# Returned ranks through PSUM, longer DMA runs, row requests four slots ahead, and SP two experts ahead in an attention and mixture-of-experts kernel

## The chip, the cores and the metric

The kernel runs on one core of a Trainium2 chip. The metric is the device time of one execution in microseconds (us); lower is better. Before the change three runs gave 371.84, 372.33 and 375.02, median 372.33 us.

## What is computed

`x` is [4, 256, 256], 1024 tokens of 256 values in all. The reference does two residual steps:

```python
x = x + xattn(layernorm(x), ctx)     # both operands rounded to fp8 by blocks of 128, then multiplied
x = x + moe(layernorm(x))            # 64 experts of width 176, top 8 for each token, and a shared expert of width 352
```

In `moe` a router scores 64 experts, keeps four of eight groups and then the eight best experts of a token. Each expert computes `silu(x Wg) * (x Wu)` and multiplies it by `Wd`; the eight results of a token are weighted and added, and the shared expert is added too.

## The kernel before, in words

The work has three parts, written as one program for each engine (SP, POOL, ACT, DVE, PE) with semaphores between them.

*Front.* Attention, layer norm, router, shared expert. The kernel then sorts tokens by expert. A token's eight experts in ascending order are its *ranks* 0 to 7. POOL scatters the token rows (256 values and 64 weights) into the DRAM buffer `xs`, rank by rank, with eight indirect DMAs a rank (line 477); after each rank it counts `ranks_in` up (line 469).

*Slot loop* (lines 591, 917, 1110). A *slot* is up to 128 rows of one expert; with these inputs there are 84 slots, in 21 groups of four (*quads*). In the iteration of slot j:

- ACT copies the transposed intermediate (594) and the high half of the rows (286), waits for SP to announce the gate/up weights (602), computes silu of slot j+1 (604), copies the high half of the weights of slot j+3 (304), and asks for the rows of slot j+AHEAD (`load_rows`, 556), if enough ranks are stored; AHEAD is 5. In the first iteration of a quad it stores the y of the quad before to `ys` (588).
- PE turns the rows of slot j+2 (1089), turns the intermediate of slot j (1120), does gate and up of slot j+1 (1095, six products) and down of slot j (1134).
- DVE makes the low halves (314, 308), multiplies silu by up (321) and scales y (930).
- SP goes by experts, in rings of four places (360 to 407). It waits until a place is free, loads the gate/up weights of the expert after, announces the gate/up weights that it loaded before, loads the down weights and announces the earlier ones. For each it reads an expert's number and a slot number into registers (361, 364).

*Tail.* POOL gathers the results of each rank back from `ys` with eight indirect DMAs (493), as soon as the last quad that holds the rank is stored, in the order of ranks. DVE adds ranks 0 to 6 to `fin`, each as one operation over 2048 columns (939), and the last rank in four quarters (944); SP stores each quarter to the output (411).

Results lie in `ys` by slot and row: `yidx` (886) holds for each token and rank its row there.

Of the kernel before, what the change touches and what calls it, by code (L numbers as in the profile page):

```python
# [5 lines left out]
def xattn_moe_kernel(  # L6
# [22 lines left out]
    I = w_down.shape[1]  # L29
# [24 lines left out]
    AHEAD = 5  # L54
    COLS = R * (QUADS + 1) + AHEAD
    ROWS = T * TOPK
    QROWS = R * P
    FILLS = QUADS * R // C
# [4 lines left out]
    with ctx:  # L63
# [93 lines left out]
        yos8 = sb("yos8", [P, C, 8])  # L157
        sidx = sb("sidx", [P, C, 8], i32)
        yidx = sb("yidx", [P, C, 8], i32)
        slot_ge = sb("slot_ge", [E, COLS])  # L160
        used_ge = sb("used_ge", [E, E + 1])
# [7 lines left out]
        used_tab = sb("used_tab", [1, E + 1], i32)  # L169
        first_tab = sb("first_tab", [1, E + 1], i32)  # L170
# [63 lines left out]
        top_ok, top_ps, max_ok, max_ps, ranks_ok = (sem(n) for n in ("top_ok", "top_ps", "max_ok", "max_ps", "ranks_ok"))  # L234
        y_sum, done = sem("y_sum"), sem("done")
# [28 lines left out]
        def load_down(eng, e, r):  # L264
            eng.dma_start(d_ring[:, r, :, :], w_down[bass.ds(e, 1), :, :].rearrange("a (s p) h -> p (a s) h", p=I0)).then_inc(d_in[r], 16)
# [5 lines left out]
        SLOT_ROWS = [(0, COLS), (COLS, COLS), (2 * COLS, E + 1), (2 * COLS + E + 1, E + 1)]  # L271
        assert 2 * COLS + 2 * (E + 1) <= 512
# [67 lines left out]
        def _(sp):  # L340
# [19 lines left out]
            def used_expert(n):  # L360
                return sp.value_load(used_tab[0:1, bass.ds(n, 1)], min_val=0, max_val=E - 1)  # L361

            def first_slot(n):
                return sp.value_load(first_tab[0:1, bass.ds(n, 1)], min_val=1, max_val=MAX_SLOTS)  # L364
# [5 lines left out]
            experts = [used_expert(r) for r in range(3)]  # L370
            for r in range(3):
                load_gu(sp, experts[r], r)
            announce(gu_in, 0, 1, gu_there)
            experts.append(used_expert(3))
            load_down(sp, experts[0], 0)
            announce(gu_in, 1, 1, gu_there)
            load_gu(sp, experts[3], 3)
            load_down(sp, experts[1], 1)
            announce(gu_in, 2, 1, gu_there)
            announce(d_in, 0, 1, down_there)  # L380
            load_down(sp, experts[2], 2)
            announce(gu_in, 3, 1, gu_there)
            announce(d_in, 1, 1, down_there)
            load_down(sp, experts[3], 3)
            announce(d_in, 2, 1, down_there)

            e, first = used_expert(R), first_slot(1)
            rings = sp.value_load(sizes[0:1, 1:2], min_val=0, max_val=E // R - 1)
            quads = quads_of(sp)
            sp.wait_ge(glo_ok, first)  # L390
            load_gu(sp, e, 0)
            with sp.Fori(0, E // R - 1) as i:
                with sp.If(i < rings):
                    e, first = used_expert(i * R + R), first_slot(i * R + 1)
                    for r in range(R):


                        e_next, first_next = used_expert(i * R + (R + r + 1)), first_slot(i * R + (r + 2))
                        sp.wait_ge(glo_ok, first_next)
                        load_gu(sp, e_next, (r + 1) % R)  # L400
                        announce(gu_in, r, i + 2, gu_there)
                        sp.wait_ge(out_ps, first)
                        load_down(sp, e, r)
                        announce(d_in, (r - 1) % R, i + (1 if r == 0 else 2), down_there)
                        e, first = e_next, first_next
            announce(gu_in, 0, rings + 2, gu_there)
# [92 lines left out]
        def _(act):  # L499
# [115 lines left out]
            store_quad(quads, bass.ds((quads + 1) % 2, 1))  # L615
# [570 lines left out]
```

## Time and profile before

| what | before |
|---|---|
| median of 3 runs | 372.33 us |
| the profiled execution | 372.08 us |
| its span, first to last instruction | 370.1 us |
| PE busy | 267.1 us (72%) |
| DVE busy | 267.0 us (72%) |
| ACT busy | 168.5 us (46%) |
| POOL busy | 165.6 us (45%) |
| slot loop, first to last y (line 930) | 113.2 to 334.4 us |
| DMA, mean over the span | 233 GB/s |

Times in the rows below are counted from the span's start. In a timeline a row has start, duration, engine, line, operation, tiles, how many were merged, and in brackets the engine's idle time before it and what ended it. An engine's name with q is its sequencer: it issues DMAs and loads registers while the engine computes. "issue" is waiting for nothing that the profile shows.

### The profile page before, as it was taken

What the parts mean: (1) busy time and instruction counts of PE and PEld (TensorE: products, weight loads), DVE (VectorE), ACT (ScalarE), POOL (GpSimd) and SP (SyncE); (2) the same over time, 40 slices, a digit from 0 to 9 for tenths busy, and PEclk for the clock granted to TensorE, in tenths of its full rate; (3) what the DMA queues carried; (4) which work ended last, traced back from release to release, by engine and by line L of the source; (5) the groups of instructions that cost most, each with busy time, mean ns of one, the idle gap of its engine ahead of it and who ended that gap; (6) DMA issues with size and microseconds to landing.
All of it is one profiled execution on the core that took longest, in us unless ns stands there. A gap on an engine that the chain in (4) does not pass through costs nothing.

```text
span 370.1 us, 7966 instructions
## 1 busy us (share of the span) xinstructions
PE 267.1 (72%) x1431; PEld 217.3 (59%) x1432; DVE 267.0 (72%) x640; ACT 168.5 (46%) x407; POOL 165.6 (45%) x164
## 2 busy tenths in 40 slices
PE   0101479979959499999999996898999989990000
PEld 0001165444748388888888885687888878880000
DVE  4799779996436268888887885565788887888832
ACT  1071542310126156667766764455676666660000
POOL 5015410427777778770000000445302773788882
PEclk9999999998979889999999999798999999997555
DMA  7999960004967479799757796898948899774134
GB/s 236 409 425 428 425 265 3 0 0 141 339 236 252 159 257 333 252 299 283 228 177 245 213 273 192 263 280 257 298 128 269 265 309 294 217 224 136 57 118 137
DMA packets 49241, 86.23 MB, mean 233 GB/s; under 512 B 5676, under 2 KB 38220, under 8 KB 47180
## 3 DMA queue, kind: packets, MB, share of 16 engines
q1 hardware_dynamic: 18652, 41.10, 32.0%
q10 hardware_dynamic: 24432, 26.12, 22.3%
q0 software_dynamic: 6144, 18.88, 15.3%
q14 instruction: 10, 0.08, 0.1%
q8 instruction: 3, 0.05, 0.1%
HBM read 46.07 MB, written 40.01 MB: 233 GB/s over the span
## 4 chain that ended last, share of the span: by engine, by line
PE 35%; DMA 13%; issue 12%; POOL 11%; DVE 10%; SPq 4%; POOLq 1%; ACT 1%; ACTq 1%; DVEq 1%
PE bank L1095 14%; PE bank L1134 13%; POOL xs L477 7%; PE bank L1120 4%; PE bank L1089 3%; DMA d_ring<-w_down 3%; DMA rows<-xs 3%; DMA early_c<-w_gu 3%; POOL xw L493 2%; POOL s_int L493 2%; SPq L361 1%; DMA xs<-xw,sidx 1%; SPq L364 1%; DVE gtop L778 1%; DMA ys<-y 1%
## 5 line engine op out<-in xcount | busy, mean ns | idle before, releaser
L1134 PE MATMUL bank<-d_ring,early_c 88*128 x336 | 93.8, 404 | 6.4 <-ACT early_c L594 5.3
L308 DVE TENSOR_TENSOR gu_lo<-early_c,gu_hi 128x704 fp32r<-128x704 f32 x87 | 76.9, 884 | 1.0 <-ACT gu_hi L304 0.6
L477 POOL DMA_INDIRECT xs<-xw,sidx x64 | 66.1, 1033 | 24.1 <-issue 23.2
L493 POOL DMA_INDIRECT early<-ys,yidx x24 | 26.2, 1094 | 102.4 <-DMA ys<-y 96.0
L1134 PEld LDWEIGHTS bank<-d_ring,early_c 88*128 88x128 f32 x336 | 60.5, 198 | 19.0 <-issue 12.6
L304 ACT ACTIVATE gu_hi<-early_c 128x704 fp32r x87 | 68.0, 782 | 5.9 <-issue 5.8
L930 DVE TENSOR_SCALAR y<-bank,rows 128x256 f32<-128x256 f32 x84 | 40.6, 483 | 34.2 <-PE bank L1134 32.7
L1095 PE MATMUL bank<-gu_hi,r_hi 128*128 128x352 f32 x170 | 63.8, 375 | 0.7 <-DVE r_lo L314 0.7
L1095 PE MATMUL bank<-gu_hi,r_lo 128*128 128x352 f32 x170 | 56.2, 331 | 0.0
L1095 PE MATMUL bank<-gu_lo,r_hi 128*128 128x352 f32 x170 | 56.1, 330 | 0.0
L594 ACT ACTIVATE early_c<-bank 88x256 f32<-88x256 f32 x84 | 31.9, 380 | 49.9 <-PE bank L1120 34.0
L604 ACT ACTIVATE early_t<-bank 128x176 f32<-128x176 f32 x84 | 26.6, 317 | 39.2 <-PE bank L1095 26.6
L314 DVE TENSOR_TENSOR r_lo<-bank,r_hi 128x256 fp32r<-128x256 f32 x86 | 36.0, 419 | 10.6 <-ACT r_hi L286 9.5
L321 DVE TENSOR_TENSOR early_t<-early_t,bank 128x176 f32<-128x176 f32 x85 | 28.5, 336 | 19.4 <-ACT early_t L604 15.2
L1089 PE MATMUL bank<-ident,rows 128*128 128x128 f32 x172 | 34.4, 282 | 6.3 <-DMA rows<-xs 5.8
L1120 PE MATMUL bank<-ident,early_t 128*88 128x128 f32 x168 | 33.8, 284 | 6.7 <-DVE early_t L321 6.4
L1089 PEld LDWEIGHTS bank<-ident,rows 128*128 128x128 f32 x172 | 24.4, 147 | 17.9 <-DMA rows<-xs 6.5
L286 ACT ACTIVATE r_hi<-bank 128x256 fp32r<-128x256 f32 x86 | 32.0, 372 | 4.4 <-PE bank L1089 4.4
L1095 PEld LDWEIGHTS bank<-gu_hi,r_hi 128*128 128x128 f32 x170 | 33.3, 196 | 1.1 <-issue 0.9
L1095 PEld LDWEIGHTS bank<-gu_lo,r_hi 128*128 128x128 f32 x170 | 33.5, 197 | 0.0
L1095 PEld LDWEIGHTS bank<-gu_hi,r_lo 128*128 128x128 f32 x170 | 33.0, 194 | 0.0
L1004 PE MATMUL bank<-xfT,sgu_sb 128*128 128x512 f32 (+1 forms) x48 | 24.9, 673 | 0.5 <-ACT scores L547 0.5
(199 smaller groups left out, 291.3 us busy)
## 6 DMA issues: line engine op xcount, KB each, us to landing
ys<-late SPq DMA_DIRECT2D x16, 1024.0 KB, 23.4
rows<-xs ACTq DMA_DIRECT2D x89, 160.0 KB, 3.3
early_c<-w_gu SPq DMA_DIRECT2D x37, 352.0 KB, 3.9
ys<-y ACTq DMA_DIRECT2D x22, 512.0 KB, 4.2
d_ring<-w_down SPq DMA_DIRECT2D x36, 176.0 KB
xc<-x SPq DMA_DIRECT2D x2, 512.0 KB, 4.0
xc<-ctx_kn SPq DMA_DIRECT2D x1, 1024.0 KB, 9.3
xs<-xw,sidx POOLq DMA_INDIRECT x64
```

What stands on the lines that cost most here:

```text
L286: act.activation(r_hi[:, b, :, :], XT[b][:, 0:H].rearrange("p (k t) -> p k t", k=KB), ACT.Copy).then_inc(rhi_ok, 1)
L304: act.activation(gu_hi[:, b:b + 1, :], gu_ring[:, bass.ds(nth % R, 1), :], ACT.Copy).then_inc(ghi_ok, 1)
L308: v.tensor_tensor(gu_lo[:, b:b + 1, :], gu_ring[:, bass.ds(nth % R, 1), :], gu_hi[:, b:b + 1, :].bitcast(fp32), ALU.subtract).then_inc(glo ...
L314: v.tensor_tensor(r_lo[:, b, :, :], XT[b][:, 0:H].rearrange("p (k t) -> p k t", k=KB), r_hi[:, b, :, :].bitcast(fp32), ALU.subtract).then_ ...
L477: pool.indirect_dma_start(out=xs, out_offset=bass.IndirectOffsetOnAxis(ap=sidx[:, c, at:at + 1], axis=0), in_=xw[:, c, :], in_offset=None, ...
L493: pool.indirect_dma_start(out=back[k][:, c, :], out_offset=None, in_=ys, in_offset=bass.IndirectOffsetOnAxis(ap=yidx[:, c, at:at + 1], axi ...
L594: act.activation(iT[:, r % 2, :, :], IT[r % 2][0:I0, 0:2 * P].rearrange("p (s t) -> p s t", s=2), ACT.Copy).then_inc(iT_ok, 1)
L930: v.tensor_scalar(y[:, odd, r, :], OB[r % 2][:, 0:H], rows[:, place, bass.ds(expert + H, 1)], None, ALU.mult).then_inc(y_ok, 1)
L1089: ins = pe.transpose(XT[b][:, k * P:(k + 1) * P], rows[:, r, k * P:(k + 1) * P], ident[:, :])
L1095: ins = pe.matmul(GB[b][:, 0:GU], r[:, b, k, :], gu[:, b, k * GU:(k + 1) * GU], start=(s == 0), stop=(s == len(parts) - 1))
L1120: ins = pe.transpose(IT[b][0:I0, s * P:(s + 1) * P], inter[:, b, s * I0:(s + 1) * I0], ident[:, :])
L1134: ins = pe.matmul(OB[b][:, 0:H], iT[:, b, s, :], d_ring[:, place, s, :], start=(s == 0), stop=(s == 1))
```

## The change

1. DRAM layouts. `w_down` is stored so that a partition reads one run of 512 values in place of two of 256. In `ys` a quad's rows lie partition by partition, so that a partition writes one run of four rows. The row of a token in `ys` then needs its slot and its quad, which `home_rows` computes on DVE just before the loop; the single operation of line 886 goes.
2. AHEAD is 4, and the request for rows stands before the copy of the weights' high half.
3. SP loads the gate/up weights of the expert after next (LEAD is 2), and reads the numbers of a ring of four with three loads of several registers. A table `gu_first_tab` is made for it on DVE.
4. The sum of the returned ranks: PE adds ranks 0 and 1 into four PSUM banks by a product with the identity; ACT copies ranks 2 to 6, in quarters, into four other banks; DVE adds the quarters from the banks to `fin`; the last rank is added from SBUF by quarters as before.

```diff
-    AHEAD = 5
+    AHEAD = 4
...
-            eng.dma_start(d_ring[:, r, :, :], w_down[bass.ds(e, 1), :, :].rearrange("a (s p) h -> p (a s) h", p=I0)).then_inc(d_in[r], 16)
+            eng.dma_start(d_ring[:, r, :, :], w_down[bass.ds(e, 1), :, :].rearrange("a p (s h) -> p (a s) h", s=2)).then_inc(d_in[r], 16)
...
+            for n in range(LEAD):
+                sp.wait_ge(glo_ok, after_slot(gu_firsts[n]))
+                load_gu(sp, number(sp, used[n]), n)
+            announce(gu_in, 0, 2, gu_there)
             with sp.Fori(0, E // R - 1) as i:
                 with sp.If(i < rings):
-                    e, first = used_expert(i * R + R), first_slot(i * R + 1)
+                    sp.load(used, used_tab[0:1, bass.ds(i * R + R, R + LEAD)])
+                    sp.load(firsts, first_tab[0:1, bass.ds(i * R + 1, R)])
+                    sp.load(gu_firsts, gu_first_tab[0:1, bass.ds(i * R + 1, R + LEAD)])
                     for r in range(R):
-                        e_next, first_next = used_expert(i * R + (R + r + 1)), first_slot(i * R + (r + 2))
-                        sp.wait_ge(glo_ok, first_next)
-                        load_gu(sp, e_next, (r + 1) % R)
-                        announce(gu_in, r, i + 2, gu_there)
-                        sp.wait_ge(out_ps, first)
-                        load_down(sp, e, r)
+                        sp.wait_ge(glo_ok, after_slot(gu_firsts[r + LEAD]))
+                        load_gu(sp, number(sp, used[r + LEAD]), (r + LEAD) % R)
+                        announce(gu_in, (r + 1) % R, i + (3 if r == R - 1 else 2), gu_there)
+                        sp.wait_ge(out_ps, after_slot(firsts[r]))
+                        load_down(sp, number(sp, used[r]), r)
                         announce(d_in, (r - 1) % R, i + (1 if r == 0 else 2), down_there)
...
-                act.dma_start(ys[bass.ds(quad * QROWS, QROWS), :].rearrange("(r p) h -> p r h", p=P),
+                act.dma_start(ys[bass.ds(quad * QROWS, QROWS), :].rearrange("(p r) h -> p r h", r=R),
...
+                    load_rows(starts[odd][r], waiteds[odd][r], (odd * R + r + AHEAD) % RING)
                     weights_high(act, nth, (r + 1) % 2)
-                    load_rows(starts[odd][r], waiteds[odd][r], (odd * R + r + AHEAD) % RING)
...
+            for k in range(PE_RANKS, TOPK - 1):
+                act.wait_ge(back_in[k], C * 16)
+                for q in range(LAST):
+                    if k > PE_RANKS:
+                        act.wait_ge(plane_sum, (k - PE_RANKS - 1) * LAST + q + 1)
+                    act.activation(bank[LAST + q][:, :].rearrange("p (c h) -> p c h", c=CL), back[k][:, q * CL:(q + 1) * CL, :],
+                                   ACT.Copy).then_inc(plane_ps, 1)
...
-            v.tensor_scalar(yidx[:, :, :], yos8[:, :, :], QROWS - 1.0, None, ALU.add).then_inc(home_ok, 1)
...
+            def home_rows():
+
+                whole(y_slot, yos8, P, -1)
+                whole(y_quad, y_slot, R, 0)
+                step(v.tensor_scalar(yos8[:, :, :], yos8[:, :, :], float(R), QROWS - float(R), ALU.mult, ALU.add))
+                step(v.tensor_scalar(y_quad[:, :, :], y_quad[:, :, :], float(QROWS - R), None, ALU.mult))
...
-            for k in range(TOPK - 1):
-                v.wait_ge(back_in[k], C * 16)
-                step(v.tensor_tensor(fin[:, :, :], fin[:, :, :], back[k], ALU.add))
-                settle()
...
+            for k in range(PE_RANKS, TOPK - 1):
+                for q in range(LAST):
+                    v.wait_ge(plane_ps, (k - PE_RANKS) * LAST + q + 1)
+                    if k > PE_RANKS:
+                        v.wait_ge(plane_sum, (k - PE_RANKS - 1) * LAST + q + 1)
+                    add_half(q, turned(LAST + q)).then_inc(plane_sum, 1)
+            for q in range(LAST):
+                v.wait_ge(low_ranks_ps, q + 1)
+                v.wait_ge(plane_sum, (TOPK - 2 - PE_RANKS) * LAST + q + 1)
+                step(add_half(q, turned(q)))
...
+            for k in range(PE_RANKS):
+                pe.wait_ge(back_in[k], C * 16)
+            for q in range(LAST):
+                for k in range(PE_RANKS):
+                    ins = pe.matmul(bank[q][:, :], ident[:, :], back[k][:, q * CL:(q + 1) * CL, :].rearrange("p c h -> p (c h)"),
+                                    start=(k == 0), stop=(k == PE_RANKS - 1))
+                ins.then_inc(low_ranks_ps, 1)
```

`whole` is two operations that round to a whole number by adding and subtracting a large constant; `home_rows` ends in two more operations that put `yidx` together.

## Rows read from the trace of the kernel before

**Rows 1.** Page, the chain that ended last, shares of the span by engine

```profile
PE 35%; DMA 13%; issue 12%; POOL 11%; DVE 10%; SPq 4%; POOLq 1%; ACT 1%; ACTq 1%; DVEq 1%
```

**Rows 2.** Timeline, one undisturbed iteration: start us, us, engine, line, op, tiles, count

```profile
328.71 0.38 PE L1089 MATMUL bank<-ident,rows 128*128 128x128 f32 x2
...
330.37 0.32 ACT L604 ACTIVATE early_t<-bank 128x176 f32<-128x176 f32 x1 [0.37 <-PE bank L1095]
...
330.88 0.34 ACTq L556 DMA_DIRECT2D rows<-xs  x1
...
330.99 0.38 PE L1089 MATMUL bank<-ident,rows 128*128 128x128 f32 x2
```

**Rows 3.** Lines 930 and 1089 in three stretches: count, ns min/median/max, first and last start

```profile
L930 DVE TENSOR_SCALAR y<-bank,rows x11: 482/483/484, 310.2 to 333.9; 128x256 f32<-128x256 f32 x11
...
L1089 PE MATMUL bank<-ident,rows x134: 270/274/421, 133.3 to 305.1; 128*128 128x128 f32 x134
...
L1089 PE MATMUL bank<-ident,rows x156: 270/274/421, 133.3 to 331.1; 128*128 128x128 f32 x156
```

**Rows 4.** DMA issues from 265 to 330 (last number: us to landing); line 556, 140 to 330

```profile
rows<-xs ACTq DMA_DIRECT2D x27, 160.0 KB, 3.3
...
DMA to landing us min/median/max: 2.1/3.7/6.1
```

**Rows 5.** Waits from 204 to 262: who waited for whom, us, times, longest

```profile
ACT early_t L604 <- SPq L368: 11.9, 7, 2.9
```

**Rows 6.** SP's and ACT's register loads (lines 361, 364, 300); line 262, 204 to 260

```profile
L361 SPq TENSOR_LOAD <-used_tab x45: 264/437/1782, 87.6 to 305.6; - x45
...
L364 SPq TENSOR_LOAD <-first_tab x41: 262/270/1342, 102.9 to 306.4; - x41
...
L300 ACTq TENSOR_LOAD <-quad_tab x69: 307/314/911, 94.3 to 331.8; - x69
...
DMA to landing us min/median/max: 3.6/4.3/6.1
```

**Rows 7.** Timeline at slot 8 and at slot 74

```profile
126.08 0.34 ACTq L556 DMA_DIRECT2D rows<-xs  x1
...
126.66 0.38 ACT L594 ACTIVATE early_c<-bank 88x256 f32<-88x256 f32 x1 [6.10 <-POOLq L469]
...
133.34 0.38 PE L1089 MATMUL bank<-ident,rows 128*128 128x128 f32 x2
...
304.94 0.44 PE L1089 MATMUL bank<-ident,rows 128*128 128x128 f32 x2 [1.09 <-DMA rows<-xs]
```

**Rows 8.** Timeline of the tail; line 493, the gathers into s_int

```profile
312.50 1.01 POOL L493 DMA_INDIRECT xc<-ys,yidx  x1 [5.45 <-DMA ys<-y]
...
333.91 0.48 DVE L930 TENSOR_SCALAR y<-bank,rows 128x256 f32<-128x256 f32 x1 [0.57 <-PE bank L1134]
...
335.88 0.42 ACTq L588 DMA_DIRECT2D ys<-y  x1
...
336.23 6.94 DVE L939 TENSOR_TENSOR x<-x,early 128x2048 f32<-128x2048 f32 x3 [1.04 <-issue]
336.40 3.02 POOL L493 DMA_INDIRECT s_int<-ys,yidx  x1 [0.30 <-issue]
...
365.93 0.69 DVE L944 TENSOR_TENSOR x<-x,xw 128x512 f32<-128x512 f32 x1 [2.15 <-DMA xw<-ys,yidx]
...
L493 POOL DMA_INDIRECT s_int<-ys,yidx x8: 1007/2018/3015, 335.1 to 351.3; - x8
```

**Rows 9.** Groups by line: count, busy us, mean ns of one, idle before

```profile
L1004 PE MATMUL bank<-xfT,sgu_sb 128*128 128x512 f32 (+1 forms) x48 | 24.9, 673 | 0.5 <-ACT scores L547 0.5
...
L830 DVE TENSOR_TENSOR pos<-bank,offset 128x512 f32<-128x512 f32 x1 | 0.7, 690 | 0.0
...
L542 ACT ACTIVATE xfT<-bank 128x512 f32<-128x512 f32 x4 | 2.3, 596 | 5.5 <-PE bank L979 5.5
...
L886 DVE TENSOR_SCALAR yidx<-yos 128x64 int32<-128x64 f32 x1 | 0.3, 317 | 0.1
```

More of the change, by code:

```diff
@@ L28, in xattn_moe_kernel @@
     E = gate_kn.shape[1]
-    I = w_down.shape[1]
+    I = 2 * w_down.shape[1]
     GU = 2 * I
@@ L358, in _, with after_slot @@
             sp.wait_ge(regs_ok, 1)
[L360 to L364, printed above, removed]
+            LEAD = 2
+            used = [sp.alloc_register(f"sp_used{n}") for n in range(R + LEAD)]
+            firsts = four_registers(sp, "sp_first")
+            gu_firsts = [sp.alloc_register(f"sp_gu_first{n}") for n in range(R + LEAD)]
+            quad_used = four_registers(sp, "sp_quad_used")
+            def after_slot(register):
+                return sp.snap(register, min_val=0, max_val=2 * P - 1) & (2 * P - 1)
             def announce(loaded, place, loads, there):
@@ L368, in announce @@
                 sp.sem_inc(there, 1)
-            experts = [used_expert(r) for r in range(3)]
+            sp.load(quad_used, used_tab[0:1, 0:R])
             for r in range(3):
-                load_gu(sp, experts[r], r)
+                load_gu(sp, number(sp, quad_used[r]), r)
+            load_down(sp, number(sp, quad_used[0]), 0)
             announce(gu_in, 0, 1, gu_there)
-            experts.append(used_expert(3))
-            load_down(sp, experts[0], 0)
+            load_gu(sp, number(sp, quad_used[3]), 3)
@@ L404, in _ @@
                         announce(d_in, (r - 1) % R, i + (1 if r == 0 else 2), down_there)
-                        e, first = e_next, first_next
-            announce(gu_in, 0, rings + 2, gu_there)
+            announce(gu_in, 1, rings + 2, gu_there)
             announce(d_in, R - 1, rings + 1, down_there)
@@ L847, in _ @@
             step(v.tensor_copy(cum_col[:, :], bank[1][0:E, CUM:CUM + 2]))
+            step(v.tensor_copy(slots[:, :], bank[1][0:1, TOTAL:TOTAL + 1]))
             step(v.tensor_scalar(quads_f[:, 0:1], bank[1][0:1, TOTAL:TOTAL + 1], 1.0 / R, (R - 1.0) / R - 0.375, ALU.mult, ALU.add))
@@ L908, in _ @@
                     weights_low(v, number(v, first_nths[f]), f, f + 1)
+            home_rows()
             quads = quads_of(v)
@@ L936, in _, with add_half, turned @@
             v.wait_ge(sh_fin, C)
-            for k in range(TOPK - 1):
-                v.wait_ge(back_in[k], C * 16)
-                step(v.tensor_tensor(fin[:, :, :], fin[:, :, :], back[k], ALU.add))
-                settle()
-            for a in range(LAST):
-                cs = slice(a * CL, (a + 1) * CL)
-                v.wait_ge(final_in[a], CL * 16)
-                v.tensor_tensor(fin[:, cs, :], fin[:, cs, :], back[TOPK - 1][:, cs, :], ALU.add).then_inc(y_sum, 1)
+            sums = [0]
+            def add_half(q, what):
+                ins = v.tensor_tensor(fin[:, q * CL:(q + 1) * CL, :], fin[:, q * CL:(q + 1) * CL, :], what, ALU.add)
+                sums[0] += 1
+                return ins
+            def turned(q):
+                return bank[q][:, :].rearrange("p (c h) -> p c h", c=CL)
+            for k in range(PE_RANKS, TOPK - 1):
[9 more added lines that the diff above has]
+            for q in range(LAST):
+                v.wait_ge(final_in[q], CL * 16)
+                if q == 0:
+                    settle()
+                add_half(q, back[TOPK - 1][:, q * CL:(q + 1) * CL, :]).then_inc(y_sum, 1)
         @block.tensor
```

61 lines of the change are left out of this document (44 added, 17 removed).

## The prediction

> **What bounds the kernel now.** I read the chain of waits first. It gives PE 35%, DMA 13%, pure issue 12%, POOL 11% and DVE 10% [rows 1], so no one engine bounds the span and it has to be taken stage by stage. Four stages matter to this change.
>
> First, the slot loop in its undisturbed form. In the timeline of one iteration PE goes from one turn of rows at 328.71 to the next at 330.99 without a gap [rows 2]. The line that scales y shows 11 executions from 310.2 to 333.9, ten slots at 2.37 us [rows 3]. PE sets that pace. A request for rows leaves ACT at 330.88, 2.17 us after its iteration's turn. It is for the slot five ahead, whose turn comes three iterations later, so it has about 4.9 us to land. The landings of these requests have a median of 3.3 us in a quiet late stretch; over the loop the line shows 2.1 / 3.7 / 6.1 us [rows 4]. Five slots ahead therefore covers nearly all of them.
>
> Second, the same loop between 204 and 262, where many experts own one slot each. The waits there put 11.9 us in 7 waits of ACT's silu down to SP's announcement of the gate/up weights [rows 5].
>
> Third, the beginning. ACT issues the request for slot 8 only at 126.08 and then goes on after 6.10 us idle, released by POOL, which has to store rank 3 first [rows 7].
>
> Fourth, the tail. The loop's last y is at 333.91, the last addition starts at 365.93. In between DVE adds planes of 2048 columns (6.94 us for three) and POOL's gathers stretch: one takes 3.02 us beside the first addition, and the eight into s_int have 1.007 / 2.018 / 3.015 us [rows 8].
>
> **The change, part by part.** The sum is made against the profiled execution: 370.1 us of span, 372.08 us of time, 1.98 around it. That is 0.25 below the median of 372.33 of the runs.
>
> *Row requests four ahead.* Nothing is added to the instructions; the request moves ahead of the weight copy and names the slot after next but two. ACT's sequencer now issues it straight behind the silu at 330.37. In the present order the request starts 0.51 after silu (330.88), with the weight copy's dispatch between them; I take 0.35, so 2.0 us after the iteration's turn at 328.71 [rows 2]. The slot it asks for is turned two iterations later, no longer three. That closes a chain in which PE waits for itself: turn, 2.0 us to the request, the landing L, 0.05 us, then the turn two slots on. Two slots cannot take less than 2.05 + L. With PE's own 2.37 a slot, the row is on time only while L stays below 2.69 us. At the quiet stretch's median of 3.3 [rows 4] the pace is (2.05 + 3.3) / 2 = 2.68 us. The bounds: at the shortest landing, 2.1, PE's 2.37 stays; at 3.7, the loop's median, 2.88; at 6.1 on every request, 4.07, which no average reaches. I take 3.3, since the stretch of 3.7 includes requests that met stalled weight loads and the scatter of ranks, and since the store to ys, which the request shares ACT's queue with, becomes a quarter as many runs. The delay that the request now puts before the weight copy (at most the request's 0.34 us plus its preparation) lies inside the 0.31 us a slot that PE then waits for rows; without that cover it is up to 0.2 us on three slots in four.
>
> *Longer runs for ys and w_down.* The bytes are the same: 512 KB a store, 176 KB a load. Nobody waits for a store inside the loop except POOL's gathers. I cost it at nothing by itself; between none and 1 us shorter landings, counted in the 3.3 above. By the Trainium skill (DMA: Bandwidth & Descriptors, Queues, rings and completion order) each DMA engine takes turns between queues packet by packet, so fewer and longer packets would give the store a larger share and let the request behind it go sooner. Going by that I would put L nearer 3.0 and the time near 355; no run here shows it yet, and the sum does not use it.
>
> *SP two experts ahead.* Four experts' numbers come in three loads of several registers in place of ten loads of one. One such load has 0.437 (experts) or 0.270 us (slots), a load of four registers 0.314 [rows 6]. Ten single loads are about 3.5 us, three multiple ones at most 1.5, so SP saves some 0.5 us an expert. More important, a gate/up request leaves one expert earlier, 2.68 us more against a landing of 4.3 us in that stretch [rows 6]. The order on SP also moves: the announcement of down weights now stands behind the landing of the next gate/up, but those are needed three slots after the gate/up of the same expert. So the 11.9 us [rows 5] go, bounded by 0 and 11.9; and a loop that runs at 2.68 throughout hides a third of that by itself. What is late next is the row, priced above. The one load that SP now issues after the last weight copy ends in the tail on an idle queue: nothing.
>
> *The index arithmetic.* home_rows puts eight small DVE operations (0.317 us is the row of the one they replace [rows 9]), about 2 us with their waits, in front of the first r_lo; six more stand before the register tables, where ACT's register loads cover them. Both end in the wait for rank 3. POOL stores that rank no later, so slot 8 is asked for at 126.08 as before [rows 7]. But it is asked for one iteration later, so the loop stands one slot further when it stops. The row lands at 126.08 + 3.3 = 129.4 and is turned then; before, slot 8 was turned at 133.34 [rows 7]. That gains 3.9 us. If the start is later than I think, less; bounds 0 and 4.5.
>
> *The loop in sum.* From the turn of slot 8 there are 156 matmuls of that line, 78 turns, so 77 slots, to 330.99 [rows 2, 3]. Before: 197.65 us, 2.57 a slot with its stalls. After: 77 x 2.68 = 206.4. The last turn comes at 129.4 + 206.4 = 335.8, the last y 2.92 later (333.91 - 330.99) at 338.7, ACT's last store 1.97 later (335.88 - 333.91) at 340.7.
>
> *The tail.* ACT copies ranks 2 to 6 by quarters of 512 columns, 0.596 us each on the nearest row, and DVE adds bank and fin at 0.690 [rows 9]. DVE is the slower. Its work: 5 ranks x 4 + 4 from PE + 4 of the last rank = 28 x 0.69 = 19.3 us, 0.5 for waits. It starts at 340.7 + 0.42 + 0.60 = 341.7 and ends at 361.5. PE's eight products are hidden: 16 passes, at the 0.67 of line 1004 [rows 9] 10.7 us, 21 if each took twice that, of some 16 before DVE asks for them; so at worst 5 more. POOL runs beside it: rank 4's gathers began at 312.50 [rows 8], 7.6 after the turn of slot 74 (304.94 [rows 7], 66 slots after slot 8, by 134 matmuls [rows 3]); now 129.4 + 66 x 2.68 + 7.6 = 313.9, and 32 gathers at 1.01 + 0.30 [rows 8] are 42 us, landing near 358. So DVE ends last, if gathers keep 1.01. That they do is the next point.
>
> Why gathers shrink: the row shows 3.02 us for one that started 0.17 us into an addition with two operands in SBUF, and 1.007 for the shortest of the same group [rows 8]; 336.40 + 3.02 = 339.42 lies 0.9 behind the end of the first of three additions of 2.3 us. The change's additions read one operand from PSUM. The Trainium skill (SBUF — State Buffer, Who interferes with whom) says that a DVE operation with two SBUF inputs holds off GpSimd's reads, but infers that tensor_tensor does not stall descriptor generation. By that inference nothing would be gained here; the trace speaks against it.
>
> Last addition's end: 365.93 + 0.69 = 366.62 before, 361.5 after, 5.1 earlier. Span 365.0, time **367.0 us**.
>
> **Rivals.**
> *Rows cost more than the rest gives (slower).* Place: PE's turn in the loop. Price: 0.1 us of landing is 0.05 a slot, 3.85 us in all. The point from which it decides: 77 x P = 366.62 - 361.5 + 206.4 = 211.5, P = 2.75, L = 3.44 us. For it: the 3.7 over the loop [rows 4], and that the spread of landings costs more than their median; against it: a slower loop loads the DMA queues less. At 3.7 the time is 367 + 77 x 0.195 = 382.
> *Rows land within 2.7 us.* The loop keeps 2.37 a slot: 24 us less than my loop, of which up to 11.9 return as waits for weights, and POOL then ends the tail; 344 to 356, say 351. Only shorter landings than most of [rows 4] do it.
> *Gathers stay long whatever DVE reads.* Place: POOL's last sixteen gathers. The longer ones would then come from sharing DMA or memory with any DVE work. Against it: the 0.9 us behind the addition's end, as worked out above; for it: additions run through the whole of POOL's last stretch. Eight of them at 2.0 put 8 us on POOL's 358, the last addition near 366.4: 371.9, no change.
>
> **How the numbers follow.** Forecast 0.47, slower rival 0.27, rows on time 0.14, gathers long 0.12. The range 355 to 381 takes in most of the first, second and fourth and the edge of the third; the forecast's own range is 361 to 373 (L from 3.14 to 3.46). A measurement of this kernel tells about 1% from no change. Faster by over 1% (below 368.6): 0.14 and seven tenths of 0.47, 0.48. Within 1%: 0.12 and the rest of the forecast, 0.25. Slower: 0.27.
>
> **What would show it.** Right: PE's turns released by DMA rows in most iterations with waits of some 0.3 us; slots near 2.68; no long wait of silu for SP; slot 8 turned near 129; gathers in the tail at 1.01; DVE busy without a break for 20 us after the last store. Wrong: slots at 2.37 with rows landed (then far faster), slots near 2.9 (then slower), or gathers of 2 us beside additions from PSUM.

## The result and the profile after

The changed kernel takes **389.38 us** (median of 4, 383.73 to 393.01) against 373.52 for the kernel before beside it: a ratio of 1.0329, 95% interval 1.0197 to 1.0462. The ratio, here and below, leaves out executions over 1.5% slower than the fastest of their kernel, the medians do not, and the profiled execution of after, 393.01 us with a span of 391.3, is one of those left out. The changed kernel is slower, and all four of its times lie above the predicted range.

Line numbers of after: turn of rows 1154 (was 1089), gate/up products 1160, weight copy gu_hi 313, silu 616, request for rows 568, y 977, additions of the tail 988.

The page of after gives the chain first, by engine and by line. DMA has gone from 13% to 23% [rows 1], and nearly all of it is the rows:

```profile
PE 26%; DMA 23%; issue 14%; POOL 10%; DVE 9%; ACTq 4%; ACT 1%; POOLq 1%; DVEq 0%
DMA rows<-xs 19%; PE bank L1160 11%; PE bank L1199 8%; POOL xs L489 5%; PE bank L1154 4%; PE bank L1185 3%; DMA xs<-xw,sidx 2%; POOL s_int L505 2%; POOL xw L505 1%; DVE gtop L797 1%; ACTq L568 1%; POOL xc L505 1%; ACTq L309 1%; POOL late L5
```

The waits of after's loop (engine, line, what it waited for: us in total, times, longest):

```profile
ACT gu_hi L313 <- issue: 41.9, 76, 0.7
PEld bank L1154 <- DMA rows<-xs: 37.7, 31, 5.1
...
PE bank L1154 <- DMA rows<-xs: 26.3, 19, 4.7
```

and of before's (from 133 to 331):

```profile
PE bank L1089 <- DMA rows<-xs: 1.5, 2, 1.1
```

PE itself stood 26.3 us for rows, in 19 waits, the longest 4.7, where it had stood 1.5. (Its weight-load half, PEld, stands in the same waits.) ACT's silu no longer waits for SP at all [rows 5]. The landings of the requests, by the line that issues them, from 140 to 362 (min/median/max):

```profile
DMA to landing us min/median/max: 2.1/2.8/7.7
```

The median is 2.8, less than the 3.7 of before [rows 4] and than the 3.3 that I took. The two medians are of different requests, though: the trace has the landings of 56 of these 74 requests, from all four places in a quad, and in before of 27 of 74, all of them of the two requests behind the store. Place by place, the request behind the store has a median of 4.36 before (9 landings) and 3.34 after (19), the next one 3.00 (18) and 3.01 (18). So the loss is still no general lateness. Here is one of the pauses, in the timeline of after (start, duration, engine, line, operation; in brackets the idle time before it):

```profile
194.92 0.37 ACTq L600 DMA_DIRECT2D ys<-y  x1
...
196.76 0.35 ACTq L568 DMA_DIRECT2D rows<-xs  x1
...
199.90 0.48 DVE L977 TENSOR_SCALAR y<-bank,rows 128x256 f32<-128x256 f32 x1 [0.17 <-PE bank L1199]
...
202.90 0.69 PE L1154 MATMUL bank<-ident,rows 128*128 128x128 f32 x2 [3.16 <-DMA rows<-xs]
...
206.23 0.34 ACTq L568 DMA_DIRECT2D rows<-xs  x1
...
207.28 0.64 PE L1154 MATMUL bank<-ident,rows 128*128 128x128 f32 x2
...
207.65 0.48 DVE L977 TENSOR_SCALAR y<-bank,rows 128x256 f32<-128x256 f32 x1 [1.08 <-PE bank L1199]
```

A quad's store leaves ACT at 194.92 and the request for slot 33 behind it, at 196.76, on the same queue. PE turns those rows 6.14 us later, at 202.90, after 3.16 us idle; the request of before would have had 2.4 us more. y of slots 30 and 31, which PE finishes two slots after it has turned them, stands at 199.90 and 207.65: this step takes 7.75 us, although the pause is only 3.16. The windows of 2 us over the same stretch (first columns: busy time of PE, PEld, DVE, ACT, POOL; PEclk is the granted clock as a share of 2.4 GHz) show the rest:

```profile
197.00:199.00 2.00, 1.97 (x13) 1.65 (x12) 1.32 (x3) 1.63 (x4) 0.00 (x0) 1.00 1.01 376
...
201.00:203.00 2.00, 0.10 (x1) 0.10 (x2) 0.43 (x1) 0.00 (x0) 0.00 (x0) 0.58 0.38 98
203.00:205.00 2.00, 2.00 (x9) 1.97 (x10) 0.19 (x1) 0.65 (x2) 0.00 (x0) 0.50 0.01 3
205.00:207.00 2.00, 2.00 (x7) 1.73 (x7) 0.57 (x2) 0.58 (x2) 0.00 (x0) 0.50 0.80 246
207.00:209.00 2.00, 2.00 (x12) 1.76 (x10) 1.28 (x2) 1.18 (x3) 0.00 (x0) 0.71 0.35 107
209.00:211.00 2.00, 2.00 (x14) 1.83 (x13) 1.25 (x3) 1.15 (x4) 0.00 (x0) 1.00 0.10 13
```

PE came out of its pause at a granted clock of 0.50, 1.2 GHz, and worked at that through the windows from 203 to 207; from 209 on it is 1.00 again. This pause cost twice: once as a wait and once as slow products. Over the whole loop, the kernel before and the changed one:

```profile
133.00:331.00 198.00, 188.63 (x1081) 164.38 (x1080) 151.23 (x308) 126.57 (x309) 76.16 (x72) 0.97 0.80 252
```

```profile
133.00:364.00 231.00, 202.66 (x1084) 169.09 (x1083) 154.90 (x310) 130.65 (x308) 81.54 (x76) 0.93 0.70 219
```

The same number of products (1081 and 1084) kept PE busy for 188.6 us at a mean clock of 0.97 before, for 202.7 at 0.93 after. Of the 33 us by which the loop grew, 14 are longer busy time of as many products and 19 idle time (9.4 to 28.3).

Not all of the 14 is the clock. Laid over the clock that the trace has for each moment, 26.3 us of PE's busy time were at 0.50, before 10.2. Gate/up products follow each other in 0.16 us at 1.00 (197.78 and 197.94) and in 0.29 at 0.50 (204.41 and 204.70), so these 16.1 us more are worth some 7 us, an estimate; the other 7 are busy time at 1.00, and no run isolates what made it. The kernel before with four ahead (run 3 below) shows that the loop can lose without the clock:

```profile
128.00:350.20 222.20, 196.31 (x1079) 161.15 (x1077) 154.16 (x310) 131.62 (x309) 82.14 (x77) 0.98 0.75 231
```

Its loop is 24.6 us longer than before's, 16.6 of that idle and 8.0 busy time, with 9.3 us at 0.50, no more than before.

The 33 us sit in few places: nine steps of y with a pause over 0.8 us of PE take 53.1 us together where nine steps of 2.5 would take 22.5; the pauses themselves are 20.7 us. Six of them end at y of slots 31, 39, 47, 51, 63 and 71, each the last of its quad, as above: the row that was late is the one requested next behind a store.

The tail, in the timeline of after:

```profile
366.45 0.48 DVE L977 TENSOR_SCALAR y<-bank,rows 128x256 f32<-128x256 f32 x1 [0.57 <-PE bank L1199]
...
367.87 8.80 PE L1210 MATMUL bank<-early,ident 128*128 128x512 f32 x16 [1.92 <-issue]
...
368.43 0.37 ACTq L600 DMA_DIRECT2D ys<-y  x1
368.84 2.15 ACT L633 ACTIVATE bank<-early 128x512 f32<-128x512 f32 x4 [2.02 <-issue]
...
369.55 14.44 DVE L988 TENSOR_TENSOR x<-x,bank 128x512 f32<-128x512 f32 x24 [1.63 <-ACT bank L633]
...
384.06 1.01 POOL L505 DMA_INDIRECT xw<-ys,yidx  x1 [0.30 <-issue]
...
387.21 0.69 DVE L988 TENSOR_TENSOR x<-x,xw 128x512 f32<-128x512 f32 x1 [1.23 <-DMA xw<-ys,yidx]
```

From the last y to the end of the last addition it takes 21.5 us (366.45 to 387.90), before 32.7 (333.91 to 366.62 [rows 8]). The eight gathers into s_int, 1.007 / 2.018 / 3.015 before [rows 8], and the last eight:

```profile
L505 POOL DMA_INDIRECT s_int<-ys,yidx x8: 1008/1012/1638, 363.7 to 373.5; - x8
L505 POOL DMA_INDIRECT xw<-ys,yidx x8: 1007/1012/1012, 374.8 to 384.1; - x8
```

### The profile page after: what moved, and what is told of

The parts are those of the page before. It is cut to its first block, busy times and chain, and to the rows that moved or that the text cites. A ratio compares the mean times of both kernels' runs of the same rounds, so it can differ in the third digit from the quotient of the medians.

```text
span 391.3 us, 7917 instructions
## 1 busy us (share of the span) xinstructions
PE 288.9 (74%) x1447; PEld 224.4 (57%) x1448; DVE 270.6 (69%) x670; ACT 183.6 (47%) x427; POOL 159.3 (41%) x164
## 4 chain that ended last, share of the span: by engine, by line
PE 26%; DMA 23%; issue 14%; POOL 10%; DVE 9%; ACTq 4%; ACT 1%; POOLq 1%; DVEq 0%
DMA rows<-xs 19%; PE bank L1160 11%; PE bank L1199 8%; POOL xs L489 5%; PE bank L1154 4%; PE bank L1185 3%; DMA xs<-xw,sidx 2%; POOL s_int L505 2%; POOL xw L505 1%; DVE gtop L797 1%; ACTq L568 1%; POOL xc L505 1%; ACTq L309 1%; POOL late L505 1%; DMA xw<-ys,yidx 1%
## 5 line engine op out<-in xcount | busy, mean ns | idle before, releaser
L1199 PE MATMUL bank<-d_ring,early_c 88*128 x336 | 97.1, 414 | 4.5 <-ACT early_c L606 3.4
L489 POOL DMA_INDIRECT xs<-xw,sidx x64 | 67.8, 1059 | 25.4 <-issue 22.9
L1199 PEld LDWEIGHTS bank<-d_ring,early_c 88*128 88x128 f32 x336 | 62.4, 203 | 20.8 <-issue 13.5
L1160 PE MATMUL bank<-gu_hi,r_hi 128*128 128x352 f32 x170 | 65.1, 383 | 3.1 <-DVE r_lo L323 3.1
L1154 PE MATMUL bank<-ident,rows 128*128 128x128 f32 x172 | 36.2, 294 | 31.2 <-DMA rows<-xs 30.9
L1160 PE MATMUL bank<-gu_hi,r_lo 128*128 128x352 f32 x170 | 57.8, 340 | 0.0
L1160 PE MATMUL bank<-gu_lo,r_hi 128*128 128x352 f32 x170 | 57.5, 338 | 0.0
L1154 PEld LDWEIGHTS bank<-ident,rows 128*128 128x128 f32 x172 | 22.8, 149 | 49.6 <-DMA rows<-xs 41.6
L606 ACT ACTIVATE early_c<-bank 88x256 f32<-88x256 f32 x84 | 31.3, 373 | 35.5 <-PE bank L1185 32.9
L330 DVE TENSOR_TENSOR early_t<-early_t,bank 128x176 f32<-128x176 f32 x85 | 28.2, 332 | 14.1 <-ACT early_t L616 11.2
L1160 PEld LDWEIGHTS bank<-gu_hi,r_hi 128*128 128x128 f32 x170 | 34.4, 203 | 3.7 <-issue 3.3
L1160 PEld LDWEIGHTS bank<-gu_hi,r_lo 128*128 128x128 f32 x170 | 34.3, 202 | 0.0
```

Of the source, the lines that this page charges most:

```text
L489: pool.indirect_dma_start(out=xs, out_offset=bass.IndirectOffsetOnAxis(ap=sidx[:, c, at:at + 1], axis=0), in_=xw[:, c, :], in_offset=None, ...
L606: act.activation(iT[:, r % 2, :, :], IT[r % 2][0:I0, 0:2 * P].rearrange("p (s t) -> p s t", s=2), ACT.Copy).then_inc(iT_ok, 1)
L1154: ins = pe.transpose(XT[b][:, k * P:(k + 1) * P], rows[:, r, k * P:(k + 1) * P], ident[:, :])
L1160: ins = pe.matmul(GB[b][:, 0:GU], r[:, b, k, :], gu[:, b, k * GU:(k + 1) * GU], start=(s == 0), stop=(s == len(parts) - 1))
L1199: ins = pe.matmul(OB[b][:, 0:H], iT[:, b, s, :], d_ring[:, place, s, :], start=(s == 0), stop=(s == 1))
```

## The experiments

All ratios are to the kernel before, run on the same chip.

**1. Five slots ahead, the rest of the change as it is.** Theory 1 (cover): the row's 2.8 us between request and turn are too little for the few long landings.

```
-    AHEAD = 4
+    AHEAD = 5
```

> The changed kernel with one constant back at its old value: rows are asked for five slots ahead again, everything else of the change stays (order on ACT, long runs, SP two experts ahead, tail through PSUM). Theory 1, cover: the loss lies only in that a request has about 2.8 us until its slot is turned while a handful of landings take 5 to 8 us; one slot more gives about 5.1 us. Then turn 8 to turn 85 falls from 230.5 us to 185 to 192 (2.4 to 2.5 a slot), PE's wait for rows from 31 us to under 6, and with the shorter tail the time is 347 to 357. Theory 2, the long store: the long packets of the store to ys hold the request behind them on the same queue; half of its cost stays, time 362 to 375, and landings over 5 us still make PE wait. Theory 3, traffic: weights two experts ahead load the queues so that rows land late whoever asks when; time 365 to 385.

Measured: 367.22 us, 0.9896 (0.9833 to 0.9958). The rows are in time again, in the groups by line of the whole run (count, busy, mean ns, idle before and its cause), first the changed kernel, then this one:

```profile
L1154 PE MATMUL bank<-ident,rows 128*128 128x128 f32 x172 | 36.2, 294 | 31.2 <-DMA rows<-xs 30.9
```

```profile
L313 ACT ACTIVATE gu_hi<-early_c 128x704 fp32r x87 | 68.8, 792 | 52.7 <-issue 48.7 <-POOLq L481 3.9
...
L1154 PE MATMUL bank<-ident,rows 128*128 128x128 f32 x172 | 34.0, 279 | 4.0 <-DMA rows<-xs 3.5 <-issue 0.3
```

PE waits 3.5 us for rows, not 30.9, though the median landing is 3.5 us here. One slot of distance is worth 1.0329 - 0.9896, 4.3% or 16 us. But turn 8 to turn 85 takes 202.1 us, not 185 to 192: theory 1 is right on the cause and wrong on what is left, and by the time alone theories 2 and 3 would do as well; runs 3 and 4 decide between them. The quickest four slots, counted from the same place of a quad (y of slot 4k+2 to the next), take 9.71 us against 9.40 before, and from y of slot 40 to y of slot 51 (the stretch that the expectations call slots 42 to 52) it is 39.5 us against 37.8. The next runs look for these two.

**2 to 4. Old order on ACT; only the rows changed in the kernel before; old runs of ys.**

```
# 2: changed kernel
+                    weights_high(act, nth, (r + 1) % 2)
                     load_rows(starts[odd][r], waiteds[odd][r], (odd * R + r + AHEAD) % RING)
-                    weights_high(act, nth, (r + 1) % 2)
# 3: kernel before
-    AHEAD = 5
+    AHEAD = 4
...
-                    weights_high(act, nth, (r + 1) % 2)
                     load_rows(starts[odd][r], waiteds[odd][r], (odd * R + r + AHEAD) % RING)
+                    weights_high(act, nth, (r + 1) % 2)
...
# 4: changed kernel
-              ys[bass.ds(quad * QROWS, QROWS), :].rearrange("(p r) h -> p r h", r=R),
+              ys[bass.ds(quad * QROWS, QROWS), :].rearrange("(r p) h -> p r h", p=P),
...
-            home_rows()
+            v.tensor_scalar(yidx[:, :, :], yos8[:, :, :], QROWS - 1.0, None, ALU.add).then_inc(home_ok, 1)
```

> The changed kernel with ACT's old order: weight copy before the request for rows, still four slots ahead. Theory 1, cover: the request leaves up to 0.5 us later, the two-slot chain grows by that, up to 0.25 us a slot where rows are late: 390 to 408, not faster than the changed kernel. Rival, order: putting the request ahead of the weight copy delays gu_hi and with it the gate/up products (gu_hi has 49.7 us of issue in front of it, gu_lo 20.8 us behind gu_hi); then this is faster than the changed kernel, 375 to 385.

> The kernel before with only the rows' distance (four) and ACT's order changed; short runs, SP one expert ahead, the old tail. Theory 1, cover: the loop loses here what it loses in the change, 2.57 to about 3.0 a slot or 77 x 0.4 = 30 us, partly covering the 11.9 us of weight waits: 392 to 405, slower than the changed kernel by up to the tail's 11 us. Theory 2 (long store) and 3 (traffic of SP two ahead): without them rows land in time often enough, 373 to 383.

> The changed kernel with the old order of rows in ys: runs of 1 KB in place of 4 KB, the old index arithmetic in place of home_rows; four slots ahead stays. Theory 1, cover: little changes, 382 to 395; long landings behind the store stay at 4 to 8 us. Theory 2, long store: requests behind the store (r=1) land near 2.5 to 3 us as the others, PE's wait for rows falls under 12 us, 360 to 372.

Measured: 385.05 us, 1.0327 (1.0255 to 1.0399); 390.34 us, 1.0521 (1.0446 to 1.0596); 386.49 us, 1.0374 (1.0310 to 1.0439). Run 3 has none of the long runs and none of SP's second expert, and has the longest time of the three, with the old tail: turn 8 to turn 85 is 222.3 us in it, against 197.65 before and 230.5 in the changed kernel, its last y 353.2. The time is just under theory 1's 392 to 405 and far over the 373 to 383 of theories 2 and 3. So distance and order alone make 24.6 of the 32.9 us that the loop lost, and theories 2 and 3 fall as the main cause. Run 4 says the same from the other side: PE waits 28.1 us for rows, not under 12. The landings,

```profile
DMA to landing us min/median/max: 2.1/2.4/4.8
```

have a lower median than with 4 KB runs only because fewer of the 38 that the trace has are of the request behind the store. That request has 3.49 (10 landings) with 1 KB runs and 3.34 (19) with 4 KB, and the kernel is no faster. Run 2 missed theory 1's 390 to 408 and touches the rival's 385, but its ratio equals the changed kernel's, so neither order wins at four ahead: where PE waits for rows, the weight copy's place is free, as predicted. The distance is enough for the loss, without the new order.

**5. Five ahead and the old order** (the edits of 1 and 2 together).

> The changed kernel with five slots ahead and ACT's old order, weight copy first; the rest of the change stays. With five ahead and the new order an undisturbed quad took 9.84 us against 9.48 in the kernel before. Theory A: the request in front of the weight copy holds gu_hi back, and PE waits for gu_lo behind it; then the quad goes back to 9.5, 18 quads save 5 to 7 us: 358 to 363. Theory B: the new order costs nothing and the slower quad comes from longer packets beside it: quads stay at 9.8, 365 to 369.

Measured: 366.30 us, 0.9752 (0.9681 to 0.9823). The median missed the 358 to 363 of theory A and lies in theory B's 365 to 369, but the mechanism of A shows in the groups by line:

```profile
L317 DVE TENSOR_TENSOR gu_lo<-early_c,gu_hi 128x704 fp32r<-128x704 f32 x87 | 76.9, 884 | 1.1 <-ACT gu_hi L313 0.6
L313 ACT ACTIVATE gu_hi<-early_c 128x704 fp32r x87 | 68.0, 783 | 5.0 <-SPq L381 5.0
```

In the run with five ahead and the new order ACT sat idle 48.7 us by "issue" in front of gu_hi, 0.5 us a slot in which its sequencer issued the request; now none, the quickest four slots go from 9.71 to 9.34 us, and turn 8 to turn 85 from 202.1 to 199.3. So the order, hidden while PE waits, costs up to 0.4 us a quad when it does not, but only 2.9 us over the 77 slots: the median of four slots stays at 9.8, as theory B said (9.82 and 9.85 over all places).

**6. SP as before, on top of 5.**

```
-            LEAD = 2
...
+            experts = [used_expert(r) for r in range(3)]
...
+                        e_next, first_next = used_expert(i * R + (R + r + 1)), first_slot(i * R + (r + 2))
```

> As the run with five ahead and the old order, and SP's part as in the kernel before: one expert ahead, two register loads of one number for each expert. Theory A: looking two experts ahead gains nothing, since SP loads 16 registers at the head of each four experts (3.0 us at the shortest) with the queues empty behind it; with the old part the waits for weights between slots 42 and 52 stay or shrink, 0 to 6 us faster than the run with SP's new part. Theory B: the second expert ahead hides landings of weights; without it the stretch is 5 to 10 us longer and the time with it.

Measured: 363.15 us, 0.9692 (0.9642 to 0.9742), and again, beside runs 9 and 10, 362.71 us, 0.9747 (0.9679 to 0.9815).

> The same kernel as the run with five ahead, ACT's old order and SP's old part, again beside the next two, for a direct comparison: 361 to 365 by every theory, 0.965 to 0.975 of the kernel before.

Looking two experts ahead shows no gain as it is written. The hole it makes, in the run with five ahead (windows of 2 us, columns as above; DMA share and GB/s last):

```profile
228.00:230.00 2.00, 1.98 (x13) 1.50 (x12) 1.71 (x4) 1.18 (x4) 0.00 (x0) 1.00 0.80 249
230.00:232.00 2.00, 2.00 (x12) 1.58 (x10) 1.46 (x3) 0.84 (x3) 0.00 (x0) 1.00 0.85 251
232.00:234.00 2.00, 0.20 (x2) 0.00 (x0) 0.00 (x0) 0.00 (x0) 0.00 (x0) 1.00 0.46 183
234.00:236.00 2.00, 0.00 (x0) 0.00 (x0) 0.00 (x0) 0.14 (x1) 0.20 (x1) 0.69 0.04 16
236.00:238.00 2.00, 1.39 (x6) 1.38 (x7) 1.03 (x3) 1.47 (x4) 1.70 (x2) 0.50 0.76 217
```

SP issued one load of weights at 228.82 and the next at 235.34. From 230.38 to 235.01 it loads its registers; the rows of the changed kernel for them, from 140 to 362:

```profile
L408 SPq TENSOR_LOAD <-used_tab x7: 890/898/2088, 175.1 to 321.9; - x7
...
L409 SPq TENSOR_LOAD <-first_tab x7: 866/867/874, 177.3 to 323.0; - x7
...
L410 SPq TENSOR_LOAD <-gu_first_tab x8: 1263/1320/2303, 138.7 to 323.9; - x8
```

Six, four and six registers take 0.9, 0.87 and 1.3 us, at times over 2; by then the queues run empty, PE stops and falls to 0.50.

**7. The tail alone in the kernel before** (semaphores, ACT's copies, PE's sixteen products and DVE's quarters of the change; nothing else).

> The kernel before with nothing but the new tail: ranks 0 and 1 summed by PE, 2 to 6 copied into PSUM by ACT, quarters of 512 columns added by DVE. The loop is that of before, the last y near 333.9. Theory A: additions that read PSUM leave POOL's gathers at 1.01 us, the last addition ends 21 to 25 us behind the last y in place of 32.7: 361 to 364. Rival: the gain in the changed kernel came from its late loop (POOL had gathered the low ranks by then) and not from the tail; then 367 to 372.

Measured: 366.46 us, 0.9762 (0.9711 to 0.9812). The loop takes 200.2 us, the tail is 27.0 us against 32.7, 5.7 less. The other 5.5 of the 11.2 in the changed kernel go with its late loop: there POOL begins the gathers into s_int at 363.68, 2.8 us ahead of the last y, here at 337.60, 2.5 behind it. The tail and the time missed theory A (21 to 25, 361 to 364), and the time is under the rival's. The end of the tail, in the timelines of DVE and of POOL:

```profile
352.61 2.48 DVE L950 TENSOR_TENSOR x<-x,bank 128x512 f32<-128x512 f32 x4
355.19 1.29 DVE L950 TENSOR_TENSOR x<-x,xw 128x512 f32<-128x512 f32 x2
357.55 0.69 DVE L950 TENSOR_TENSOR x<-x,xw 128x512 f32<-128x512 f32 x1 [1.06 <-DMA xw<-ys,yidx]
...
353.41 1.01 POOL L495 DMA_INDIRECT xw<-ys,yidx  x1 [0.30 <-issue]
354.73 1.01 POOL L495 DMA_INDIRECT xw<-ys,yidx  x1 [0.30 <-issue]
356.04 1.33 POOL L495 DMA_INDIRECT xw<-ys,yidx  x1 [0.30 <-issue]
357.67 1.45 POOL L495 DMA_INDIRECT xw<-ys,yidx  x1 [0.30 <-issue]
```

Beside the four additions that read bank and fin (352.61 to 355.09) a gather takes 1.01 us. Two that start while an addition of the same size with two operands in SBUF runs take 1.33 and 1.45, and both end 0.89 us behind the end of that addition: 356.48 to 357.37, 358.24 to 359.12. So the operand decides and not the length of the addition, as the prediction had it from one row of before. The start counts too: the gather at 354.73 keeps its 1.01, though such an addition begins 0.46 us into it (355.19). The 1.64 in the changed kernel fits: that gather starts at 363.68 inside gu_lo (363.54 to 364.43), which also reads two operands in SBUF, and ends 0.89 behind it.

**8. The store one request later** (four ahead).

```
-                    if r == 0:
+                    if r == 1:
                         act.wait_ge(y_st, i * 16 + 32)
```

> The changed kernel, four slots ahead, with ACT's store of a quad moved from behind the first request of an iteration to behind the second, so that another request follows it. Theory A: a request is late because it stands behind the 512 KB store on its queue; the long landings move with the store from the request of r=1 to that of r=2, and the time stays within 2% of the changed kernel, 382 to 394. Theory B: what makes r=1 late is the traffic of weights at that place, not the store; long landings stay with r=1.

Measured: 391.79 us, 1.0441 (1.0368 to 1.0514). In the changed kernel the recorded landings of the request behind the store (19 of them) have a median of 3.34 us, of the next one (18) 3.01, of the one after (9) 2.43. With the store moved, the request now behind it (9) has 3.54, the one now ahead of it (19) 2.45. The long steps of y move too, from the last of a quad to the first: slots 8, 16, 20, 36 and 64, though pauses of 0.98 and 0.82 us are left at 31 and 39. Between 42 and 52 they stay, beside the weights. Theory A holds for most of the rest of the loop. The Trainium skill (DMA: Bandwidth & Descriptors, Queues, rings and completion order) says that a DMA engine takes the descriptors of one queue in ring order; this run agrees, with these medians beside it.

**9 and 10. From run 6: old runs of ys; from run 5: SP's numbers one at a time. 12: in blocks, behind requests in flight.**

```
# 9: on run 6, the edit of 4
# 10: on run 5, in the loop over r
+                        e, first = used_expert(i * R + (R + r)), first_slot(i * R + (1 + r))
...
+                            g, gf = used_expert(i * R + (R + LEAD + r + 1)), gu_first(i * R + (1 + LEAD + r + 1))
# 12: on run 5, behind load_gu and load_down of r == 0 or r == R - 1
+                            sp.load(used, used_tab[0:1, bass.ds(i * R + R, R)])
+                            sp.load(firsts, first_tab[0:1, bass.ds(i * R + 1, R)])
...
+                            sp.load(gu_used, used_tab[0:1, bass.ds(i * R + (2 * R + LEAD), R)])
...
+                            sp.load(gu_firsts, gu_first_tab[0:1, bass.ds(i * R + (1 + LEAD + R), R)])
```

> That kernel with the old order of rows in ys and the old index arithmetic, so of the change only the tail, the longer runs of w_down and the six small operations of the register tables stay. Theory A: long runs of ys are worth nothing to the loop, and home_rows costs 2.4 us at the first y (116.5 in the changed kernel, 114.1 with the old index arithmetic) which slot 8's wait for rank 3 swallows; the same time, within 2 us of the kernel beside it. Theory B: the long runs pay (half the packets of the store, cheaper loop in the stretch from slot 42 to 52); 3 to 8 us slower.

> Five ahead, ACT's old order, and SP two experts ahead as in the change, but its numbers are loaded one by one while a transfer of weights is under way, in place of 16 registers at the head of each four experts. Theory A: the hole at the head of a group (DMA share 0.0 at 235 and at 252 in the run with five ahead) was what made looking ahead worthless; without it slots 42 to 52 take 32 to 36 us in place of 37.7 to 39.7, and the time is 2 to 5 us under the kernel with SP's old part. Theory B: that stretch is bound by the bytes of weights, rows, stores and gathers together; the hole's work is only shifted, slots 42 to 52 take 37 to 40 us, and the time is within 2 us of it.

> Five ahead, ACT's old order, SP two experts ahead, its 16 registers of a group still loaded in blocks of four (0.87 us each), but each block behind a weight request that is still in flight, and none at the head of a group. Theory A: the hole at the head of a group (3.0 us and more without a transfer of weights) ate what looking ahead gives; slots 42 to 52 take 30 to 35 us against 35 to 38 with the old part, and the ratio to before is 0.955 to 0.967. Theory B: the stretch is bound by the bytes of weights, rows, stores and gathers; 35 to 38 us, ratio 0.968 to 0.980, no gain over the old part.

Measured: run 9 365.53 us, 0.9812 (0.9738 to 0.9885); run 10 375.56 us, 1.0043 (0.9987 to 1.0100); run 12 362.33 us, 0.9741 (0.9659 to 0.9824). Run 9 against its neighbour (362.71): 2.8 us lie between the two theories, and the intervals overlap, so whether the long runs of ys pay is open, at most a few us. Run 10 is a clear miss of both theories: four single loads an expert keep SP busy, its gate/up requests stand some 4 us apart (at 235.0, 239.5, 243.5 and 247.4) where a slot needs 2.4, and slots 42 to 52 take 43.2 us. In run 12 no window of this stretch has a DMA share under 0.39 (0.04 in the hole above), and those slots take 35.0, at the edge of theory A. But with SP's old part they take 37.7 and 36.3 in the two runs of that kernel and 35.1 in run 9, and the ratio is theory B's: looking ahead shows no gain here either. Whether the bytes or SP set this stretch now, the runs do not settle.

The best kernels of the study are run 6 and run 12, 362 to 363 us, 2.5 to 3% under the kernel before: the change without the request too close or in front of the weight copy, and with SP's old part or with its register loads behind requests in flight. The new tail alone (run 7) is 2.4% under it, and the intervals overlap. So the tail is the only part of the change that is shown to gain.

## Why the prediction was wrong

By its own three terms, from the trace: turn of slot 8 at 132.96 (predicted 129.4, +3.6); turn 8 to turn 85 230.5 us (206.4, +24.1); from the last turn's y to the last addition's end 21.5 us (338.7 to 361.5 = 22.8, -1.3). Together +26.4, and the span is 391.3 against 365.0.

**Four ahead: the step that failed.** "At the quiet stretch's median of 3.3 [rows 4] the pace is (2.05 + 3.3) / 2 = 2.68 us." In this pace a slot is PE's own 2.37 and a wait for rows of 0.31, over 77 slots 182.5 and 23.9 us. Measured from turn 8 to turn 85: PE busy 202.2, 2.63 a slot, waits for rows 26.3, other idle time 2.0. So the term that was too small is PE's own 2.37, by 19.7 of the 24.1 us. I had it from an undisturbed stretch; over its whole loop the kernel before was busy for 188.3, 2.45 a slot.

The wait came out near its 23.9, but by luck, since two errors met: L was taken too long, and its spread was left out. The chain was the right one: turns wait for rows, two slots cannot take less than 2.05 + L. The value put into it was wrong in kind. A pace that is the larger of two times is not found by its median: a landing of 2.1 gives nothing back, since PE's own 2.37 stays, and one of 6.1 costs all of its excess. The median then was 2.8, which by the same formula makes 4 us of waits in all and is far on the good side of my deciding point of 3.44, and the kernel is slower all the same. The row I cited for the loop had its maximum beside it, 6.1 [rows 4], and I argued that no average reaches it. The rule as it stands (a turn comes no sooner than PE's own time after the one before, and no sooner than 2.05 + L after the one before that), with L drawn at random from after's 56 landings, place by place, gives 218 us at 2.37 a slot, and 228 with 25 of waits at the measured 2.63, both estimates. Measured: 230.5 and 26.3.

**What had no term at all: longer busy time.** 13.9 us more than before for the same products, some 7 of them the clock; in the other kernels with four ahead 4.8 to 12.9 more (193.1, 196.3, 199.6 and 201.1 us in runs 2, 3, 4 and 8), with five ahead at most 3.5 more (191.8 in run 1). No rival priced it.

**The slower rival** named the right place and mechanism; its 382 from a level 3.7 was 7 low, with the same 2.37 in it. **Rows in time** is what five ahead gives, but not its 351.

**Order.** The request left 2.0 us after the turn, as said, and cost nothing beside waits (run 2); "up to 0.2 us on three slots in four without that cover" was some 0.1 a slot in the quickest quads and 0.04 over the loop (run 5).

**Longer runs.** Costed at nothing: for ys the runs do not speak against it (4, 9); w_down's runs were never taken out alone. By the rule of the Trainium skill that I had weighed (DMA: Bandwidth & Descriptors, Queues, rings and completion order) long packets would have brought the request forward; 3.49 us behind a store of 1 KB runs and 3.34 behind one of 4 KB (run 4, changed kernel) show no such gain.

**SP two ahead.** That the 11.9 us go came out, but for a poor reason: slots that wait for rows hid them, as it seems, for with rows in time they came back (from 204 to 262 12.7 us of waits for SP in the run with five ahead, 8.5 of ACT and 4.2 of PE). The three loads "at most 1.5" took 3.0 at the least, twice that term: I had taken ACT's row for four registers, 0.314 [rows 6], for SP's six and four.

**Index arithmetic.** The first y came 3.3 us later (116.5), 2.4 of it home_rows (114.1 in run 4); slot 8's request left at 129.21 and not at 126.08. "POOL stores that rank no later" failed by 3.1. POOL's scatters of that rank ended only about 1 us later, and in run 4, with the old index arithmetic and the old runs of ys, the request left at 126.64: these two edits account for 2.6 of the 3.1, though not through what.

**Tail.** 24 additions in 14.44 us, sixteen products hidden (8.80 us), gathers at 1.01 but for one: as predicted. Against my reading, the Trainium skill (SBUF — State Buffer, Who interferes with whom) infers that tensor_tensor doesn't stall descriptor generation; run 7 sides with the trace of before: 1.01 beside additions from PSUM, 1.33 and 1.45 for gathers that start while the same addition with two operands in SBUF runs.

## What to carry to other kernels

Where a request is just in time, put the whole list of landings into the recurrence, not a median, and ask what share lies above the cover; one more slot of distance was worth 4 to 6% here, and cost a buffer that was there. Take an engine's own pace from its busy time over the whole loop and not from its best stretch; here that was 2.45 against 2.37 before any change. Take out the parts of a change one by one: here one of four carried the gain. A sequencer's register loads count, most of all where they stand together in front of its next request.

## What was unexpected of the hardware

Behind a pause of 3.16 us PE worked at a granted clock of 0.50 from 203 to 207, so the step of y that held it lost 5.3 us over a usual one of 2.45. Loads of several registers on SP had medians of 0.87 us for four and of 0.9 and 1.3 for six, single ones of 0.27 and 0.44, ACT's of four 0.314. A request on ACT's queue directly behind a 512 KB store had a median landing about 1 us longer than those two and three requests later (3.34 against 2.43 and 2.38), with runs of 4 KB, and as much with runs of 1 KB (3.49 against 2.37 and 2.31). An indirect gather of POOL that began well inside a DVE operation with two operands in SBUF ended 0.89 us behind that operation's end; one that began before such an operation kept its 1.01 (354.73 in run 7).
